# One fp32 value product and one exponential in place of split value products, and a second score pass over all 128 rows

## The reference

```
qn = rmsnorm(q, qn_g) * SCALE            # 4 heads of 64, 1024 queries
kn = rmsnorm(k, kn_g)                    # 1024 + 64 keys: the rows, then the context
attn = einsum('bhid,bhjd->bhij', qn, kn)
attn = where(full_mask, attn, -max)      # masks context keys
attn = softmax(attn)
out  = einsum('bhij,bhjd->bhid', attn, v)
x = x + tanh(g_xattn) * (out @ Wo.T + bo)
probs = softmax(xf @ w_router); two largest of 8 experts for each row
h = gelu(xf @ w1[e] + b1[e]);  out = h @ w2[e] + b2[e], weighted sum
x = x + tanh(g_ffn) * out
```

## Time and profile before

| | |
|---|---|
| median of 3 runs | 1214.55 us |
| the profiled execution, its span | 1218.7 us |
| PE busy | 1021.0 us, 84% |
| weight loads (PEld) busy | 828.1 us, 68% |
| VectorE busy | 784.3 us, 64% |
| ScalarE busy | 688.7 us, 57% |
| GpSimd busy | 382.1 us, 31% |
| attention stages, from their first score product to the last | 66 to 166 us, 231 to 341, 409 to 520, 588 to 699 |

### The profile page before, as it was taken

How to read it: one execution, slowest core, us unless ns; L and a number is a source line. 1 busy time by engine, 2 the same in 40 slices (tenths; PEclk the granted TensorE clock), 3 DMA queues, 4 the chain that set the end, 5 groups by cost and what they waited for, 6 DMA issues and landing times. The chain is left out here.

```text
span 1218.7 us, 20071 instructions
## 1 busy us (share of the span) xinstructions
PE 1021.0 (84%) x5940; PEld 828.1 (68%) x5940; DVE 784.3 (64%) x1603; ACT 688.7 (57%) x1084; POOL 382.1 (31%) x275
## 2 busy tenths in 40 slices
PE   4689986699976798975898950799999999999992
PEld 4546565565665565654565650699999999999992
DVE  5946778666769565869574555366757575775751
ACT  4867758576848476848576811344544445463530
POOL 3510205316106234106242105134334343452321
PEclk9979999699989699999698975799999999999997
DMA  3010001101000100010110015324244242442325
GB/s 104 1 37 1 1 0 36 37 14 57 1 26 9 36 35 35 0 35 0 34 52 17 0 35 169 108 48 112 46 115 119 43 117 43 117 111 49 43 35 155
DMA packets 44964, 61.93 MB, mean 51 GB/s; under 512 B 7265, under 2 KB 38753, under 8 KB 44865
## 3 DMA queue, kind: packets, MB, share of 16 engines
q0 software_dynamic: 17520, 33.27, 12.2%
q1 hardware_dynamic: 27408, 28.29, 7.9%
HBM read 37.34 MB, written 28.39 MB: 54 GB/s over the span
## 5 line engine op out<-in xcount | busy, mean ns | idle before, releaser
L1500 PE MATMUL psH<-xT_hi,Q 128*128 128x256 f32 x1120 | 205.5, 282 | 10.8 <-DVE Q L1426 9.3
L1513 PE MATMUL psY<-K,g_hi 128*128 128x256 f32 x1120 | 203.3, 283 | 0.0
L1357 POOL DMA_INDIRECT total<-y_out,token_i x70 | 114.2, 1631 | 230.3 <-PE psH L1500 188.8
L1500 PEld LDWEIGHTS psH<-xT_hi,Q 128*128 128x128 f32 x1120 | 175.3, 190 | 12.5 <-issue 12.5
L1513 PEld LDWEIGHTS psY<-K,g_hi 128*128 128x128 f32 x1120 | 171.6, 188 | 0.0
L1500 PE MATMUL psH<-xT_lo,Q 128*128 128x256 f32 x560 | 157.6, 281 | 0.0
L1513 PE MATMUL psY<-K,g_lo 128*128 128x256 f32 x560 | 157.2, 281 | 0.0
L1390 ACT ACT_TABLE_LOAD x35 | 44.9, 1283 | 170.2 <-PE psH L1500 170.2
L1390 ACT ACTIVATE g<-psH,b_col 128x256 f32<-128x256 f32 x280 | 113.8, 473 | 30.6 <-DVE g_lo L1454 27.6
L630 ACT ACTIVATE p_ring_hi<-psS,shift 128x1024 fp32r<-128x1024 f32 x80 | 89.3, 1116 | 60.5 <-PE psS L1170 56.5
L472 POOL TENSOR_TENSOR rr<-ssm,minus_half 128x8 f32<-128x8 f32 (+1 forms) x36 | 60.0, 1666 | 194.5 <-DVE ssm L720 194.5
(11 more groups left out here) (226 smaller groups left out, 2182.9 us busy)
## 6 DMA issues: line engine op xcount, KB each, us to landing
lnf<-routed SPq DMA_DIRECT2D x35, 258.0 KB, 2.7
xr<-in_L_ffn_w POOLq DMA_DIRECT2D x7, 1024.0 KB
xn<-in_L_ffn_w POOLq DMA_DIRECT2D x7, 1024.0 KB
xr<-in_x SPq DMA_DIRECT2D x4, 1024.0 KB, 5.3
total<-xb SPq DMA_DIRECT2D x4, 1024.0 KB, 4.5
routed<-pad_rows SPq DMA_DIRECT2D x8, 258.0 KB
total<-y_out,token_i POOLq DMA_INDIRECT x70, 3.9
routed<-big,slot_i POOLq DMA_INDIRECT x64
```

The lines of the kernel that those rows point to most:

```text
L1357: pool.indirect_dma_start(total, bass.IndirectOffsetOnAxis(ap=token_i[:, m:m + 1], axis=0), y_out[:, m, :], None, bounds_check=NTOK + TM - ...
L1500: ins = pe.matmul(o, l, r, start=(n == 0), stop=(n == len(parts) - 1))
L1513: ins = pe.matmul(psY[m][:, 0:D], l[:, c, cols], r[:, c, :], start=(c == 0 and n == 0), stop=(c == HC - 1 and n == 2))
```

## The change

Probabilities and values are kept in fp32 (`p_ring`, three tiles, and `V`) and multiplied unsplit: `values(i)` has one product for each half. There is one exponential for each step, no subtraction, no `V_lo`, and no second copy of the context's values. `values(i)` waits for `exp_done`, and `project(t)` for `proj_read` where it waited for `v_ready`. `V` is zeroed in the lower 64 rows of the context tile. The second score product runs over all 128 rows: `K2` has a full plane for each head, filled with zeros once, of which only the 64 partitions opposite q lo are written. The diff, without the lines that only rename or declare semaphores:

```diff
--- before.py
+++ after.py
...
@@ -159,11 +158,9 @@
             ssm = sb("ssm", [P, 2, 8])
             rr = sb("rr", [P, 2, 8])
             qkd = sb("qkd", [P, 2, 2 * QK])
-            K2 = sb("K2", [P, H // 2, S + P], F32R)
-            V_hi = sb("V_hi", [P, KT, H // 2 * 3 * DH], F32R)
-            V_lo = sb("V_lo", [P, KT, H // 2 * 3 * DH], F32R)
-            p_ring_hi = sb("p_ring_hi", [P, 2, S], F32R)
-            p_ring_lo = sb("p_ring_lo", [P, 2, S], F32R)
+            K2 = sb("K2", [P, H, S + P], F32R)
+            V = sb("V", [P, KT, H // 2 * 3 * DH])
+            p_ring = sb("p_ring", [P, NP_RING, S])
             st2 = sb("st2", [P, T, 6])
             mv2 = sb("mv2", [P, T, 2])
             var2 = sb("var2", [P, T])
...
@@ -318,21 +308,6 @@
                 pairs = lambda c: ps[keep, c:c + H // 2 * n].rearrange("p (h n) -> p h n", h=H // 2)
                 return pairs(0), pairs(H // 2 * P), slice(t * P, t * P + n)
 
-            def wait_probabilities(eng, b, i):
-
-                before = sum(k < i for k in POOL_LO)
-                if i in POOL_LO:
-                    eng.wait_ge(p_ready_pool, b * len(POOL_LO) + (before + 1))
-                else:
-                    eng.wait_ge(p_ready, b * (NI - len(POOL_LO)) + (i - before + 1))
-
-            def probabilities_lo(eng, b, i):
-                p = P if i % KT < T else SC
-                eng.wait_ge(exp_done, b * NI + (i + 1))
-                hi = p_hi[i % NP_RING]
-                lo = p_lo[i % NP_RING] if i % KT < T else hi[SC:2 * SC, :]
-                return eng.tensor_tensor(lo[0:p, :], p_f32[i % 2][0:p, :], hi[0:p, :].bitcast(F32), ALU.subtract)
-
             def normed_row(eng, b, t):
 
                 if t % HT == 0:
@@ -448,8 +423,11 @@
                 pool.affine_select(out=tri[:], in_=tri[:], compare_op=ALU.is_gt, fill=0.0, base=0,
                                    pattern=[[1, P]], channel_multiplier=-1).then_inc(ident_ready, 1)
                 for a, value in ((wst_c[:, :, DC:2 * P], 0.0), (cn[:, DC:2 * P], 0.0), (lc_hi[:, :, SC:P], 0.0), (lc_lo[:, :, SC:P], 0.0),
-                                 (K1[:, :, S + SC:S + P], 0.0), (K2[:, :, S + SC:S + P], 0.0), (V_hi[:], 1.0), (V_lo[:], 0.0)):
+                                 (K1[:, :, S + SC:S + P], 0.0), (K2[:], 0.0), (V[:], 1.0)):
                     pool.memset(a if a.dtype == F32 else a.bitcast(F32), value).then_inc(pool_const, 1)
+                pool.wait_ge(pool_const, NPOOL - 1)
+                pool.memset(V[SC:P, T, :], 0.0).then_inc(pool_const, 1)
+                pool.wait_ge(pool_const, NPOOL)
                 pool.iota(iota_i[:, 0:8], [[1, 8]], base=0, channel_multiplier=0).then_inc(iota_done, 1)
                 pool.iota(iota_i[:, 8:16], [[P, 8]], base=0, channel_multiplier=1).then_inc(iota_done, 1)
                 pool.iota(tile_i[:], [[1, NTILES]], base=0, channel_multiplier=0).then_inc(iota_done, 1)
@@ -496,18 +474,12 @@
                         pool.sem_inc(passed, 1)
                     pool.tensor_copy(rows[1][:, :, 0:D], rows[0][:, :, 0:D]).then_inc(y2_ready, 1)
 
-                def cut_probabilities(b, steps):
-                    for i in steps:
-                        probabilities_lo(pool, b, i).then_inc(p_ready_pool, 1)
-
                 norm_root(0)
                 head_roots(0, False)
                 pool.wait_ge(dve_const, 5)
                 pool.wait_ge(seq_loaded, 48)
                 residual(0)
-                cut_probabilities(0, POOL_LO[0:2])
                 norm_root(1)
-                cut_probabilities(0, POOL_LO[2:])
                 with pool.Fori(1, B) as b:
                     head_roots(b, True)
                     pool.wait_ge(x2_stored, b * 16)
...
@@ -562,15 +532,13 @@
                         if t < T:
                             act.activation(qk_sb[:, t % 3, :], o[:, 0:QK], ACT.Copy)
                             act.activation(sq[:, t % 2, :], o[:, 0:QK], ACT.Square)
-                            act.activation(value_slots(V_hi, t, P), o[:, QK:QK + H * DH].rearrange(
+                            act.activation(value_slots(V, t, P), o[:, QK:QK + H * DH].rearrange(
                                 "p (i s d) -> p i s d", i=2, s=2), ACT.Copy).then_inc(proj_read, 1)
                         else:
                             act.activation(qk_sb[0:SC, t % 3, 0:H * DH], o[0:SC, 0:H * DH], ACT.Copy)
                             act.activation(sq[0:SC, t % 2, 0:H * DH], o[0:SC, 0:H * DH], ACT.Square)
-                            for rows_of in (slice(0, SC), slice(SC, 2 * SC)):
-                                ins = act.activation(value_slots(V_hi[rows_of], t, SC), o[0:SC, H * DH:2 * H * DH].rearrange(
-                                    "p (i s d) -> p i s d", i=2, s=2), ACT.Copy)
-                            ins.then_inc(proj_read, 1)
+                            act.activation(value_slots(V, t, SC), o[0:SC, H * DH:2 * H * DH].rearrange(
+                                "p (i s d) -> p i s d", i=2, s=2), ACT.Copy).then_inc(proj_read, 1)
 
                     def heads_hi(t):
                         act.wait_ge(qkT_done, b * NT + (t + 1))
@@ -627,10 +595,7 @@
                         act.wait_ge(s_done, b * NI + (i + 1))
                         if i >= NP_RING:
                             act.wait_ge(av_done, b * NI + (i - NP_RING + 1))
-                        act.activation(p_hi[i % NP_RING][0:p, :], scores_psum(i)[0:p, :], ACT.Exp, bias=bias).then_inc(p_hi_done, 1)
-                        if i >= 2:
-                            wait_probabilities(act, b, i - 2)
-                        act.activation(p_f32[i % 2][0:p, :], scores_psum(i)[0:p, :], ACT.Exp, bias=bias).then_inc(exp_done, 1)
+                        act.activation(p_ring[0:p, i % NP_RING, :], scores_psum(i)[0:p, :], ACT.Exp, bias=bias).then_inc(exp_done, 1)
                         if with_router and i == 1:
                             router_exp(b - 1)
                         if i in (24, 25):
@@ -719,10 +684,6 @@
                         dve.wait_ge(ss_ready, b * NT + (t + 1))
                         dve.tensor_scalar(ssm[0:p, t % 2, 0:n], ss[0:p, t % 2, 0:n], 1.0 / DH, RMS_EPS * RMS_EPS, ALU.mult,
                                           ALU.max).then_inc(ssm_ready, 1)
-                        v0 = QK if t < T else H * DH
-                        dve.tensor_tensor(value_slots(V_lo, t, p),
-                                          psO[t % 2][0:p, v0:v0 + H * DH].rearrange("p (i s d) -> p i s d", i=H // 2, s=2),
-                                          value_slots(V_hi, t, p).bitcast(F32), ALU.subtract).then_inc(v_ready, 1)
 
                     def scale_heads(t):
 
@@ -746,7 +707,7 @@
                                 dve.scalar_tensor_tensor(
                                     out=Q1[other, odd:H:2, cols], in0=q_src, scalar=gqk[keep, 0:1],
                                     in1=Q1[keep, odd:H:2, cols].bitcast(F32), op0=ALU.mult, op1=ALU.subtract)
-                            ins = dve.tensor_tensor(K2[keep, :, cols], k_src, K1[keep, odd:H:2, cols].bitcast(F32), ALU.subtract)
+                            ins = dve.tensor_tensor(K2[keep, odd:H:2, cols], k_src, K1[keep, odd:H:2, cols].bitcast(F32), ALU.subtract)
                         ins.then_inc(qk_ready, 1)
 
                     for t in range(NT + 2):
@@ -799,9 +760,6 @@
                                           ALU.subtract).then_inc(att_ready, 1)
 
                     for i in range(NI):
-                        if i not in POOL_LO:
-                            probabilities_lo(dve, b, i).then_inc(p_ready, 1)
-
                         h, kt = divmod(i, KT)
                         if h >= 1 and kt in (2, 4):
                             denominators(h - 1, kt // 2 - 1)
@@ -1093,7 +1051,7 @@
                         if with_router and t < 2:
                             pe.wait_ge(x2_ready, b * T)
                         if t >= 2:
-                            pe.wait_ge(v_ready, b * NT + (t - 1))
+                            pe.wait_ge(proj_read, b * NT + (t - 1))
                         o = psO[t % 2]
                         if t < T:
                             cols = slice(t * P, (t + 1) * P)
@@ -1165,29 +1123,22 @@
                         for n in range(2):
                             pe.matmul(scores_psum(i)[:, n * HALF:(n + 1) * HALF], K1[:, h, keys], Q1[:, h, n * HALF:(n + 1) * HALF],
                                       start=True, stop=False)
-                        rows_hi = slice(0, DH) if h % 2 == 0 else slice(DH, P)
                         for n in range(2):
-                            ins = pe.matmul(scores_psum(i)[:, n * HALF:(n + 1) * HALF], K2[rows_hi, h // 2, keys],
-                                            Q1[rows_hi, h, n * HALF:(n + 1) * HALF], start=False, stop=True)
+                            ins = pe.matmul(scores_psum(i)[:, n * HALF:(n + 1) * HALF], K2[:, h, keys],
```

(18 more changed lines are left out.)

5 lines of the change are left out of this document (removed).

## The result

| | before | after |
|---|---|---|
| median of 4 runs each, us | 1214.23 (1212.41 to 1215.90) | 1157.67 (1156.07 to 1158.14) |
| span of the profiled execution, us | 1218.7 | 1154.5 |

The ratio is 0.9534, with a 95% interval of 0.9521 to 0.9547: 56.6 us less in the medians, 64.2 us less in the two profiled spans. The forecast was 1190, its range 1166 to 1219. The direction was right. The size was wrong, by more than the range allowed. (A timed run reads 1.6 to 1.8 us more than the span of the same execution. So the profiled execution before was some 6 us slower than its median, and the one after 1.6 us faster; the spans overstate the gain by the 7.6 us between 64.2 and 56.6.)

What follows compares the result with a forecast made beforehand. TensorE was taken as the bound, other engines having slack. Terms: +7 (values and scores) - 4 (context steps) - 3 (stage starts) - 14 (GpSimd stall) - 10 (fronts) = -24 us, from 1214.55 to 1190 us; range 1166 to 1219.

Steps and rivals of the forecast that it cites:

- Part 1: Value products in attention steps: six fp32r instructions become two fp32 products, four instructions at 0.46 us, 1.84 us a step.
- rivals 1 and 3: Value products: 1, weight load not hidden, 1250 us, chance 15%; 3, one stream an instruction, 1069 us, chance 6%.
- the lower bound: Value products: 0.427 us an fp32 instruction, 1024 columns at 2.4 GHz; step 2.63 us, -11 us in place of +7.
- The start of a stage: First steps of each attention stage at half clock: score-only steps cheaper, steps with values dearer; -3 us (-5 to 0).
- Part 2: Second score pass over 128 rows: with fp32 values, step 2.76 against 2.71 us, +7; context steps -4, half-clock steps -3.
- The row switches: Attention steps on TensorE: going from 128 to 64 rows and back costs 0.39 us a step, which goes.
- The context steps: Steps with a context tile and those behind become like all others: 0.31 us, 12 times, -4 us.
- Part 3: One exponential, no subtraction: GpSimd's subtractions behind indirect stores no longer stall TensorE; -14 us, between -4 and -17.
- The rival that the slow steps stay: Mid-stage: ScalarE's pauses and others' gaps keep the clock falling; gain only -4 us, time 1200 us; chance 13%.
- Part 4: Fronts ahead of the attention stages: V_lo leaves VectorE, 0.34 us a tile; together -10 us (-4 to -11).
- Part 5: Constant fills at the start: V_lo's goes, K2's grows, hidden behind a weight DMA; 0 us, 1 us if uncovered.

Runs made afterwards that it cites:

- The 64-row run: The changed kernel with its second score product back over 64 rows; 1228.60 us, ratio 1.0141 to the kernel before.
- the split run with 128 rows: The kernel before, its three-product fp32r values kept, with its second score product over all 128 rows; 1181.99 us, ratio 0.9759.
- the split kernels: Kernels with the value products of the kernel before; those with all products over 128 rows and GpSimd's subtractions late or on VectorE: 1138.89 and 1128.52 us.
- the padded run: The changed kernel with 32 waits for exp_done and 32 unread one-column operations added to VectorE's program of a sequence; 1189.70 us, 13.5 more than its control.

## Why the prediction was wrong

**The fp32 instruction (Part 1): mechanism right, size off.** Two records, two streams each, load hidden: as forecast, and rivals 1 and 3 are out. The size was 0.429 to 0.430 us, not 0.46. I carried the 0.017 us by which fp32r exceeds 512 columns over to fp32 twice; it does not go with the columns. Four records make 0.12 us a step, some 15 us over 125 warm steps. This alone turned the term from +7 to -8, and it was the lower bound that I had named and not taken. It is the term that was mis-sized, as the start of a stage, next, is the step that was wrong.

**The start of a stage (Part 2): the step that failed.** The term was -3 us, "a little less because the clock may then rise later in the work". It was -18.1. I priced each product at the half clock and left the time at which the clock rises where it was. The profile shows two levels, and which one the router's 6.99 us are paid at was the larger question: at full clock they are 3.84 or less. The 64-row run puts the 7.00 back, and the split run with 128 rows takes it away without any fp32 product. So in stages 1 to 3 it is the 64-row score products that keep the clock low, with either kind of value product (with 128 rows the first four steps take 13.6 to 14.9 us with fp32 values, 13.6 to 14.3 with split ones). In stage 0 the value products, or their waits, have a part too. The Trainium skill, "TensorE: Matmul & The Clock Gate", section What's actually happening, has the clock follow how busy the engine was; here it was busy for the whole of 12 us at a granted clock of 0.50, and with the same busy time and 128 rows the clock was 0.72. Read with the profile's busy time, that rule gives no difference between the two, and the measurement decides. I had the rows of both levels in the earlier trace rows and asked only what a product costs at each, not what moves the change between them.

**The row switches (Part 2).** 0.39 us a step was read off and came back in both runs: right. The context steps are like all others, right.

**GpSimd's stall (Part 3): right in the profile, not in the timed runs.** -14 was forecast. The profile has 15.8, the timed runs without the subtractions 4.5: I took the stall of one long execution as that of the median, when I carried the 4.2 us between the two over unchanged. Of the excess of 17 us read there, some 0.8 was the context steps' own, which Part 2 counted as well. The rival that the slow steps stay was wrong in the run that was forecast; on two other chips the changed kernel has pauses of ScalarE of up to 11 us and takes 1172 and 1176. The earlier trace rows showed their small form, and I held that one exponential a step makes them harmless. A pause of 8 us outlasts the two steps by which the scores run ahead. The ratio to the kernel before is 0.958 to 0.959 there in place of 0.953, since that kernel is slower too.

**The fronts (Part 4): V_lo right, a second term missed.** V_lo's 3.0 us a gap is shown from both sides. The other 7.7 us of the gaps go with VectorE's pause at the head of passes 2 and 3, which the padded run brings back with +8.6. That row stood in the trace of before; I looked at busy shares in the fronts and not at idle time with no releaser.

**Constants (Part 5)** cost nothing that shows: TensorE's first turn still waits for the weights, until 11.7 us, and stage 0 starts 1 us earlier, within the 64.7 to 68.5 us over which that start varies between runs. (K2's fill had 128 columns before, not 256.)

Against the forecast's own terms the starts gave 15.1 us more, the later steps 17.0 (15 of it the fp32 record), the gaps 6.5, the ends 1.6: 40 us in the spans, 32 in the medians, with one sign. The range's low end summed the ends of terms that I had, and the start of a stage had no end at which the clock rises earlier.

## What to carry to other kernels

Where a clock has two levels, price a change at the start of a busy stretch twice: what each instruction costs at the level shown, and what the whole stretch would cost if the level rose earlier. Keep every product on the full 128 rows, with zeros in the unused ones, if the engine is the bound: the 64-row products streamed the same 512 columns, and the switches cost 0.39 us a step. An unsplit fp32 product was dearer than three fp32r ones (1.72 us against 1.39 a step here), so it pays only where it takes a wait away, and here the same wait goes by giving the subtractions to an engine with slack. A stall read in one profile is priced for that execution; set the profile's time beside the timed runs before it goes into a sum. When a change shortens an engine's loop body, look for "issue" pauses at the loop's head and for packets of the instruction queue.

## What the runs showed of the hardware that was not expected

- An fp32 record of 512 columns repeats every 0.429 to 0.430 us, 0.002 to 0.003 above 1024 columns at 2.4 GHz; an fp32r product every 0.23, 0.017 above 512.
- Second score products over 64 rows in place of 128 cost 0.39 us a warm step, and with them the full clock comes to stay 15 to 23 us into stages 1 to 3, in place of 1 to 13.
- 32 one-column operations and their waits in VectorE's loop cost 8.6 us of gaps, with a pause of 2.4 to 2.5 us at the loop's head in passes 2 and 3.
- While indirect stores were in flight ScalarE, which touches none of their data, stood for 3 to 11 us; on one chip the changed kernel had none of it in its profile, on two others it had it in each of stages 1 to 3, and the split kernels on the same chips had none.
